# High halves of the odd y tiles: ScalarE's copies or VectorE's casts

## The reference

```
x = x + ffn(cond(x))

ffn(x):  h = layernorm(x) * gamma + beta
         y = silu(h @ w1 + fc1_bias)      # 512 rows x 2048
         z = y @ w2 + fc2_bias            # 512 rows x 512
         return x + 0.5 * z
```

## Time and profile before

| | us |
|---|---|
| median of 3 runs | 1369.19 (1367.98 to 1369.76) |
| the profiled execution | 1367.41 |
| its span, first to last instruction | 1365.6 |

### The profile page before, as it was taken

The page is one execution under the profiler, slowest core; times in us unless marked ns, Lnnn a source line. Parts: engine busy times, 40 slices in busy tenths (PEclk is TensorE's granted clock), DMA queues, the critical chain, the costliest instruction groups (busy, mean ns, idle before and its releaser), DMA issues.

```text
span 1365.6 us, 20228 instructions
## 1 busy us (share of the span) xinstructions
PE 1299.8 (95%) x5923; PEld 1008.9 (74%) x5923; DVE 1018.5 (75%) x1998; ACT 1019.1 (75%) x1661; POOL 200.9 (15%) x164
## 2 busy tenths in 40 slices
PE   7897999999999999999999999999999999999998
PEld 5565877777777777777777777777777777777787
DVE  7899678687767868678686777868777686877725
ACT  3675777777777777777777777777787777777775
POOL 3303011030301203011030301203021020301100
PEclk9999999999999999999999999999999999999999
DMA  7852113131230313213131230313213131230100
GB/s 231 221 193 32 62 16 67 43 62 63 35 92 1 62 63 58 69 16 73 36 62 64 33 92 1 62 63 55 70 18 69 40 62 62 38 87 1 31 32 31
DMA packets 272987, 84.28 MB, mean 62 GB/s; under 512 B 248778, under 2 KB 249444, under 8 KB 272356
## 3 DMA queue, kind: packets, MB, share of 16 engines
q1 hardware_dynamic: 272208, 82.70, 25.2%
q10 hardware_dynamic: 660, 0.08, 0.0%
HBM read 51.21 MB, written 16.85 MB: 50 GB/s over the span
## 4 chain that ended last, share of the span: by engine, by line
PE 80%; DVE 12%; ACT 4%; issue 3%; DMA 1%; ACTq 0%; DVEq 0%
PE y_ps L1182 16%; PE z_ps L1211 15%; PE y_ps L1183 14%; PE z_ps L1214 14%; PE z_ps L1213 10%; DVE scratch L920 2%; PE a_ps L1141 1%; DVE z_ps L973 1%; PE a_ps L1143 1%; PE a_ps L1142 1%; PE a_ps L1093 1%; PE a_ps L1092 1%; PE a_ps L1146 1%; PE a_ps L1094 1%; ACT y_ps L655 1%
## 5 line engine op out<-in xcount | busy, mean ns | idle before, releaser
L655 ACT ACTIVATE y_ps<-y_ps,ratio 128x512 f32<-128x512 f32 x768 | 475.9, 659 | 178.2 <-PE y_ps L1183 176.1
L1211 PE MATMUL z_ps<-w_hi,y_hi 128*128 128x512 f32 x1024 | 413.0, 403 | 31.2 <-DVE z_ps L973 30.6
L1182 PE MATMUL y_ps<-hT_hi,w 128*128 128x512 f32 x1016 | 406.4, 400 | 15.2 <-DVE hT_lo L939 11.7
L1214 PE MATMUL z_ps<-w_hi,y_lo 128*128 128x512 f32 x1024 | 400.7, 391 | 0.0
L1183 PE MATMUL y_ps<-hT_lo,w 128*128 128x512 f32 x1016 | 397.4, 391 | 0.0
L964 DVE TENSOR_TENSOR y_lo<-y_f,y_hi 128x512 fp32r<-128x512 f32 x256 | 187.5, 732 | 239.9 <-ACT y_hi L566 239.4
L1213 PE MATMUL z_ps<-w_lo,y_hi 128*128 128x512 f32 x704 | 274.6, 390 | 0.0
L1211 PEld LDWEIGHTS z_ps<-w_hi,y_hi 128*128 128x128 f32 x1024 | 193.0, 188 | 100.3 <-DVE z_ps L973 30.9
L649 ACT ACTIVATE y_f<-y_ps,vec_cols,mant 128x512 f32<-128x512 f32 x256 | 187.5, 777 | 104.8 <-PE y_ps L1183 90.8
L1182 PEld LDWEIGHTS y_ps<-hT_hi,w 128*128 128x128 f32 x1016 | 191.4, 188 | 86.6 <-ACT y_ps L655 34.3
L491 POOL TENSOR_TENSOR x<-x,scratch 128x512 f32<-128x512 f32 x64 | 91.6, 1433 | 972.1 <-ACT scratch L627 972.0
(11 more groups left out here) (209 smaller groups left out, 1164.7 us busy)
## 6 DMA issues: line engine op xcount, KB each, us to landing
x<-in_x_dram SPq DMA_DIRECT2D x64, 256.0 KB, 3.4
out_dram<-x SPq DMA_DIRECT2D x64, 256.0 KB, 2.7
x_cols<-in_x_dram SPq DMA_DIRECT2D x240, 64.0 KB, 2.2
h_cols<-scratch SPq DMA_DIRECT2D x224, 64.0 KB, 2.1
fc_codes<-in_L_ffn_fc_q_dram SPq DMA_DIRECT2D x8, 1024.0 KB, 12.1
fc_scaled<-units_dram SPq DMA_DIRECT2D x4, 1024.0 KB, 16.9
e<-powers_dram SPq DMA_DIRECT2D x3, 1024.0 KB, 15.1
h_rows<-powers_dram SPq DMA_DIRECT2D x1, 1024.0 KB, 12.1
```

What stands on the lines that cost most here:

```text
L655: nc.scalar.activation(y_ps[k % 2][:], y_ps[k % 2][:], ACT.Copy, scale=ratio[:, c * NF + k:c * NF + k + 1]).then_inc(scaled, 1)
L1182: mm(o, w, hT_hi[:, c, :], start=(c == 0), stop=False, skip_group_check=True)
L1211: mm(z_ps[r][:], y_hi[k % 2][:, rows], w2_hi[:, k, :], start=(k == 0), stop=False, skip_group_check=True)
L1214: last = mm(z_ps[r][:], y_lo[k % 2][:, rows], w2_hi[:, k, :], start=False, stop=(k == NF - 1 or k in WHOLE), skip_group_check=True)
```

## The change

Odd tiles' high halves are cast by VectorE itself in `split_y`, right ahead of the subtraction; the cast takes over the two waits that ScalarE's copy had, and the subtraction waits for the cast through a new semaphore `yhi_odd`. ScalarE keeps the even tiles, and `yhi_done` now counts 8 per batch (NH) instead of 16 (NF).

```diff
@@ block.scalar, ffn @@
                     for ahead, name, n in cond_steps(b, i, ACT_PLAN, ACT_TURN, ACT_MOVED):
                         steps[name](b + ahead, n)
-                    if i % 4 == 0:
-                        y_hi_part(b, i // 2 + 1)
@@ block.vector @@
             def split_y(b, k):
-                dve.wait_ge(yhi_done, b * NF + k + 1)
+                if k % 2 == 0:
+                    dve.wait_ge(yhi_done, b * NH + k // 2 + 1)
+                else:
+                    dve.wait_ge(silu_done, b * NF + k + 1)
+                    if k >= 2 or not is_first(b):
+                        dve.wait_ge(fc2_done, b * NF + (k - 1))
+                    v.tensor_copy(y_hi[k % 2][:], y_f[k % 2][:]).then_inc(yhi_odd, 1)
+                    dve.wait_ge(yhi_odd, b * NH + k // 2 + 1)
                 v.tensor_tensor(y_lo[k % 2][:], y_f[k % 2][:], f32(y_hi[k % 2][:]), ALU.subtract).then_inc(split_done, 1)
```

More of the change, by code:

```diff
@@ L251, in build @@
         yhi_done = sem("yhi_done")
+        yhi_odd = sem("yhi_odd")
         split_done = sem("split_done")
```

## The result

| | before | after |
|---|---|---|
| median of 3 runs, us | 1369.19 | 1404.09 (1395.26 to 1405.10) |
| ratio of times, 95% interval | | 1.0237 (1.0173 to 1.0302) |
| profiled execution, us | 1367.41 | 1404.09 |
| its span, us | 1365.6 | 1402.3 |
| granted TensorE clock over the span, of full speed | 0.996 | 0.973 |

The account below looks back on a forecast made before the run. TensorE, busy 95%, was taken as the bound, so only its waits counted. 14 × (1.41 − 0.28 − 0.49) = 9.0, and 0.5 for batch 0, gave +9.5 us, or 1378.7 us; range 1363.5 to 1390.

Parts of the forecast that it names:

- Slot 17/18: GpSimd's addition gets in between cast and low half of tile 9, delaying the z rescaling and TensorE: +1.41 us per batch.
- The z bank's wait some 3.1 us: Sign in slot 18: L1211's wait for L973 would rise from 1.65 to some 3.1 us.
- The rival in which the low half keeps its turn: GpSimd doesn't get in at the gap, slot 18 costs 0.45 us per batch: −5.1, 1364.1 us; chance 0.20.
- Slot 11: Without ScalarE's copy of tile 5 the activation TensorE's weight load waits for starts 0.29 us earlier: −0.28 us per batch.
- Slots 26 to 30: VectorE no longer waits for the copy of tile 15, so the last h_lo comes earlier: −0.49 us net per batch.
- the foreseen small stall in slot 26: The cast ahead of low half 13 makes TensorE wait 0.3 us, swallowed by the wait at slot 30.
- Batch 0: Block of tile 11 +1.41, a cast ahead of slot 10's stall +0.45, slot 17 −1.4: sum +0.5 us.
- The gain foreseen at slots 17/18: In batch 0, slot 17, the cast can go before GpSimd starts instead of waiting for ScalarE: −1.4 us.
- The block of tile 11: In batch 0's h chain, slot 20/21, same order of cast, low half and ready GpSimd addition: +1.41 us.
- Passed on to L973, to TensorE: The low half's delay of 1.41 us in slot 17/18 reaches the z rescaling, TensorE and that slot's second activation.
- Parts with one answer: Whole kernel: 128 copies leave ScalarE, 80 us less; 128 casts join VectorE, 54 us more; neither bounds by its sum.
- the first rival: The low half keeps its turn at slot 18: 14 × −0.32 = −4.5, batch 0 −0.6, so 1364.1 us; chance 0.20.

Follow-up runs that it names:

- e1: Changed kernel, with GpSimd's additions held until the low half of tile 9 is made; 1381.14 us.
- e8: Changed kernel, with the cast of tile 9 (tile 11 in batch 0) moved earlier, to slot 16 after the last `LN`; 1385.15 us.
- e2: Changed kernel, with seven matmuls that nobody reads put ahead of the wait in slot 18 (slot 22 in batch 0); 1399.25 us.
- e4: Changed kernel, with three long-fulfilled waits in place of each removed ScalarE copy, so 345 instructions stand ahead of its loop as before; 1397.76 us.
- e3: Changed kernel, with tile 9 (tile 11 in batch 0) copied by ScalarE as before, the other odd tiles cast by VectorE; 1361.81 us.
- e5: Changed kernel, with only tiles 5 and 15 cast by VectorE and the other odd tiles copied by ScalarE as before; 1359.49 us.
- e9: Changed kernel with e4's waits on ScalarE, e1's wait on GpSimd and five fill matmuls in slot 18 from batch 2 on; 1361.52 us.
- e10: e5 with four fill matmuls in slot 18 from batch 2 on; 1354.62 us.

## Why the prediction was wrong

**The direction was right, the size was not**: forecast +9.5 us with a range up to 1390, measured 1404.09. Step by step:

- **Slot 17/18, right.** Low half over 1.6 us: 1.63. Its cast 0.42: 0.42. L500 at 1.25 to 1.3: 1.31. The z bank's wait some 3.1 us: 3.04. In the seven batches in which the clock doesn't fall within slot 18 itself the slot is longer by 1.38 to 1.41 us, for a forecast of 1.41. The Trainium skill's rule of the exclusive lock on the port pair (SBUF — State Buffer, "Who interferes with whom") holds here in the order that the prediction gave it; the trace agrees: e1 takes GpSimd away, e8 puts the low half ahead of it, and both times it is 0.69 us again. The prediction laid the block to the pause ahead of the low half; slot 13 of after shows the same block without a pause, so that part of the reason isn't borne out. The rival in which the low half keeps its turn fell with it.
- **Slot 11, right**: −0.29 us per batch in the mean for a forecast of −0.28, −4.0 in all.
- **Slots 26 to 30, right**: −0.52 per batch for a forecast of −0.49, −7.3 in all, with the foreseen small stall in slot 26 (+0.25) swallowed in it.
- **Batch 0**: +1.8 for a forecast of +0.5; the prologue ahead of it is 0.8 us shorter, which makes the +1.1 of the ledger. The gain foreseen at slots 17/18 (−1.4) is there with −1.92, which holds a fall of the clock that before has in this slot and after hasn't. The block of tile 11 is +1.42 in slot 22, for +1.41; slots 23 and 24 add 1.19, in which the clock stands at half (from 125.3 us on for 10.2 us, in before from 129.6 on for 3.4).
- **The step that failed: what a longer stall costs.** "Passed on to L973, to TensorE", says the prediction, and takes the stall at its own length, 1.41. It never asked what TensorE's clock does when it stands still for 3.4 us instead of 2.0, and no rival had it. The block is 14 × 1.40 = 19.6 us; slots 18 and 19–21 together came to 24.0 + 17.2 = 41.2. The other 21.6 us are the clock, 1.8 in the mean of 12 falls (1.2 to 2.8). e2 shows it: the same block, the stall half filled, 19.9 and 0.0. The trace of before had the case itself. The earlier trace rows ends at TensorE's 1.90 us of idle time ahead of 111.94, in batch 0. Behind it, from 112.5 to 115.9, the clock is at half; the first of these rows is a matmul there, the second the clock behind a stall of 4.43 us in slot 22:

```profile
113.26 0.63 PE L1211 MATMUL z_ps<-w_hi,y_hi 128*128 128x512 f32 x1
...
129.60:133.00 3.40, 3.40 (x8) 2.73 (x9) 3.40 (x4) 1.12 (x3) 3.40 (x3) 0.50 0.00 0
```

So gaps of 2.28 and 4.43 us, start to start, had a fall behind them where the 2.04 us of the middle batches had none, and the change made those 3.4.
- **The second miss: "Parts with one answer".** Taking copies off ScalarE was priced as time saved. It also makes ScalarE's program shorter, and 5.6 us went at the loop's returns. e4 shows that it isn't the missing work. The trace of before has no such row, but the program's loop was there to be seen, and where its instructions lie is something the change moved.

The sum, as measured: 19.6 + 21.6 + 5.6 − 4.0 − 7.3 + 1.1, and 0.1 in the other stretches, 36.7 us. With the two terms it lacked, the prediction's own sum would have been 9.5 + 21.6 + 5.6 = 36.7; that it meets the measured sum to the tenth is chance, as its small misses cancel. (In the first rival's sum batch 0 is 0.45 + 0.45 − 1.4 = −0.5, not −0.6.)

**What stays open.** Why ScalarE's gap comes with 314 instructions ahead of the loop and not with 318, 337 or 345, and TensorE's with 1004 and not with 990, wasn't settled; with them the loop's own length changed too. The Trainium skill (Runtime: NRT & Kernel Launch, "Instruction fetch mechanics") says that a taken branch whose target isn't at hand forces a fetch before execution goes on; a dependence on where the loop starts fits that. The third packet behind each return in the kernels with the pause agrees with it, but that it carries ScalarE's instructions isn't shown. For TensorE's pauses in e2 the fetch is only argued. Nor is it settled what decides, at one and the same gap, whether the clock falls, when, and whether for 3.41 or 6.83 us.

## What to carry to other kernels

Price a longer stall of TensorE with the clock in it: read the gap's length, start to start, and the granted clock behind it, and where a gap can't be removed, put matmuls in it. Move work between engines only at the places where a wait of the bound engine ends on it; here two tiles of eight carried all of the gain, and one all of the block. Splitting an operation of VectorE into two makes a boundary, and that is where a waiting GpSimd addition gets in; look at what GpSimd has ready there.

## What the runs showed of the hardware

- **The clock falls with gaps of 2 to 3.4 us, in some batches and not in others.** TensorE's gap from start to start in slot 18, and the batches of 14 with a fall: 2.02 to 2.12 us, none in before's profile, 4 in e3's and 2 in e5's; 2.49 us, 9 in e1's; 2.77 us, 9 in e8's; 3.43 us, 12 in after's and 14 in e4's. With matmuls put in, so that 1.86 (e2), 1.35 (e9) or 1.12 us (e10) are left, none, though in e2 TensorE's wait from the last `fc1` matmul is as long as in after. A fall starts between 1.0 us before the gap's end and 1.7 us behind it, lasts 3.41 or 6.83 us, and cost 1.8 us in the mean in after.
- **GpSimd gets in between two VectorE operations, with or without a pause.** An addition that became ready while VectorE's cast ran went ahead of the low half behind it, after a pause of 0.03 us (1.63 us for 0.69 in after); one that became ready while a low half ran went ahead of the next cast, without any pause (1.52 us for 0.42, slot 13 of after). An addition that became ready 0.23 us after a low half's start waited for it (1.59 us for 1.28, e8).
- **Where a loop lies can cost time at each return.** 31 instructions fewer ahead of ScalarE's loop (314) brought pauses of up to 1.5 us at the loop's five returns, 27 fewer (318, e3) none; 14 more ahead of TensorE's loop (e2) brought pauses of up to 2.6 us.
